# One residual block of four conditional layers on one core: the third matrix's pieces loaded ahead of the ring's blocks, table stores spread over two units, the last sum of U2 D3 moved, and the first couple's plain product cut into parts of 136 and 256 columns

## The reference

```
x = x + x W0^T + 2 * sum over the top 2 of 8 experts of gate_e * (x A_e^T) B_e^T
x = x + (per sequence of 64 tokens: C^T x, C a 64x64 matrix chosen by an id)
x = x + (x B2[id]^T) A2[id]^T            (rank 16, one of 64 adapters)
x = x + x W3^T + b + 2 * (x A3[id]) B3[id]   (rank 16, one of 32 adapters)
```

## Time and profile before

| | |
|---|---|
| median of three runs | 892.26 us |
| profiled execution | 890.0 us, its span 888.2 us |
| VectorE, ScalarE, GpSimd busy | 693.1, 379.6, 243.6 us |
| mean granted TensorE clock | 0.989 of full |
| HBM traffic | 193 GB/s over the span |

### The profile page before, as it was taken

How to read it: one execution, slowest core, us unless ns; L and a number is a source line. 1 busy time by engine, 2 the same in 40 slices (tenths; PEclk the granted TensorE clock), 3 DMA queues, 4 the chain that set the end, 5 groups by cost and what they waited for, 6 DMA issues and landing times.

```text
span 888.2 us, 15396 instructions
## 1 busy us (share of the span) xinstructions
PE 865.9 (97%) x4572; PEld 798.4 (90%) x4572; DVE 693.1 (78%) x1900; ACT 379.6 (43%) x859; POOL 243.6 (27%) x343
## 2 busy tenths in 40 slices
PE   8989999999999998899999999999999999999997
PEld 7868788888888887799999999999999999999997
DVE  5894444665565724799999999999999999999996
ACT  5562333344445732434434434434434345345343
POOL 1410100000001114415415415425325325335230
PEclk9989999999999998999999999999999999999999
DMA  7718666669687765546666655666566566566564
GB/s 260 262 61 187 173 184 167 192 187 304 226 277 241 175 166 113 155 149 185 192 181 182 196 180 183 182 185 189 173 174 194 173 188 193 174 185 186 180 189 144
DMA packets 120969, 166.24 MB, mean 187 GB/s; under 512 B 33718, under 2 KB 80566, under 8 KB 120886
## 3 DMA queue, kind: packets, MB, share of 16 engines
q1 hardware_dynamic: 120886, 165.26, 62.9%
HBM read 128.78 MB, written 42.73 MB: 193 GB/s over the span
## 4 chain that ended last, share of the span: by engine, by line
PE 72%; DVE 17%; issue 4%; DMA 3%; ACT 2%; SPq 2%; POOL 1%; DVEq 0%; POOLq 0%
PE ps_w L2125 12%; PE ps_d L2046 10%; PE ps_d L2125 10%; PE ps_o L2024 9%; PE ps_d L2117 8%; PE ps_o L2046 8%; PE ps_o L2138 4%; DVE stat_lo L1482 4%; PE ps_d L2132 3%; PE ps_s L2024 2%; PE ps_o L2162 2%; DVE CT_raw L1497 1%; PE ps_w L2132 1%; DVE rows_lo L1482 1%; DVE spare_f L1794 1%
## 5 line engine op out<-in xcount | busy, mean ns | idle before, releaser
L1482 DVE TENSOR_TENSOR stat_lo<-stat_raw,stat_hi 128x512 fp32r<-128x512 f32 (+1 forms) x150 | 148.9, 1008 | 56.2 <-ACT stat_hi L1026 46.3
L1026 ACT ACTIVATE stat_hi<-stat_raw 128x512 fp32r<-128x512 f32 (+1 forms) x150 | 115.5, 789 | 73.6 <-DVE stat_raw L1500 41.2
L875 POOL TENSOR_TENSOR stat_raw<-stat_raw,ident 128x128 f32<-128x128 f32 x36 | 25.0, 697 | 266.5 <-DMA stat_raw<-stat 266.5
L2117 PE MATMUL ps_d<-w_hi,stat_hi 128*128 128x392 f32 x256 | 87.2, 341 | 0.8 <-DVE y_lo L1482 0.8
L2117 PE MATMUL ps_d<-w_hi,stat_lo 128*128 128x392 f32 x256 | 87.0, 340 | 0.0
L2117 PE MATMUL ps_d<-w_lo,stat_hi 128*128 128x392 f32 x256 | 86.9, 340 | 0.0
L918 POOL TENSOR_TENSOR w_lo<-mdraw,w_hi 128x512 fp32r<-128x512 f32 x32 | 41.7, 1304 | 160.7 <-ACT w_hi L1026 160.7
L2024 PE MATMUL ps_o<-chunk_hi,stat_hi 128*128 128x512 f32 x168 | 65.7, 391 | 1.0 <-DVE stat_lo L1482 0.5
L2024 PE MATMUL ps_o<-chunk_hi,stat_lo 128*128 128x512 f32 x168 | 65.4, 389 | 0.0
L2024 PE MATMUL ps_o<-chunk_lo,stat_hi 128*128 128x512 f32 x168 | 65.4, 389 | 0.0
L1026 ACT ACTIVATE rows_hi<-rows_raw 128x512 fp32r<-128x512 f32 x52 | 32.6, 627 | 59.0 <-DMA rows_raw<-u 28.6
(11 more groups left out here) (284 smaller groups left out, 2520.8 us busy)
## 6 DMA issues: line engine op xcount, KB each, us to landing
up<-tu SPq DMA_DIRECT2D x124, 256.0 KB, 4.3
stat_raw<-x SPq DMA_DIRECT2D x33, 512.0 KB, 3.2
mdraw<-t SPq DMA_DIRECT2D x120, 136.0 KB, 2.4
out<-outb SPq DMA_DIRECT2D x30, 512.0 KB, 4.3
stat_raw<-stat SPq DMA_DIRECT2D x52, 256.0 KB, 3.2
stat_raw<-stat SPq DMA_DIRECT2D x26, 512.0 KB, 5.0
rows_raw<-x SPq DMA_DIRECT2D x30, 256.0 KB, 3.2
chunk_raw<-mov SPq DMA_DIRECT2D x24, 256.0 KB, 6.0
```

Of the source, the lines that this page charges most:

```text
L875: return nc.gpsimd.tensor_tensor(out=own, in0=own, in1=ident[:, :], op=ALU.add)
L1026: return nc.scalar.activation(dst, src, ACT.Copy)
L1482: return nc.vector.tensor_tensor(out=dst, in0=src, in1=rounded.bitcast(F32), op=ALU.subtract)
L2117: last = nc.tensor.matmul(plain_bank(t)[:, 0:WCOLS], rows[a][:, k, :], w[c][:, k, :], start=k == 0 and m == 0, stop=k == KB - 1 and m == l ...
```

## The change

M3's pieces are issued at the groups 0, 1 and 2: eight, four and four, each time behind the ring's block. Its steps are spread from group 0 on: ten of the twelve over the groups 0 to 6, and in group 0 and 1 the ring's blocks are split two at once; from group 2 on the block of two groups later is split, on VectorE and ScalarE, ahead of the group's steps. The language bias (`languages`) goes from before the groups to after unit 1. The stores of the D3 table are issued two before and two after the loads of A12 and A22, at unit 0 and again at unit 1; `store_mb(2)` goes to unit 1; the twelve `store_own` go to units 2 and 3, three before and three after. The last sum of U2 D3 is a function of its own, `hidden_total`, called a few instructions later.

In the first couple the plain product of each tile is made as `heads` (136 columns) and `others` (256 columns), each of 24 matmuls, so that heads need nothing from the tables. Two of the sums S of the first couple are kept in rooms of their own, and no longer wait for the table's stores (`st_md[1]`). The order on all engines is new:

```diff
-    M3_EACH = 3
+    M3_LOADED = [8, 12, 16]
-    M3_AT_GROUP = {2: M3_STEPS[0:1], 3: M3_STEPS[1:3], 4: M3_STEPS[3:5], 5: M3_STEPS[5:6], 6: M3_STEPS[6:8], 7: M3_STEPS[8:10]}
-    M3_IDENTITIES = {1: 0, 3: 1, 4: 2, 5: 3}
+    M3_AT_GROUP = {0: M3_STEPS[0:2], 1: M3_STEPS[2:3], 2: M3_STEPS[3:4], 3: M3_STEPS[4:6], 4: M3_STEPS[6:7], 5: M3_STEPS[7:9],
+                   6: M3_STEPS[9:10]}
+    M3_IDENTITIES = {0: 0, 1: 1, 2: 2, 3: 3}
...
-                for n in range(g * M3_EACH, min((g + 1) * M3_EACH, len(M3_PIECES))):
-                    load_m3(n)
+                if g < len(M3_LOADED):
+                    for n in range(M3_LOADED[g - 1] if g > 0 else 0, M3_LOADED[g]):
+                        load_m3(n)
...
-                if u == 0:
-                    for n in range(STORES):
-                        store_md(2, n)
-                    store_mb(2)
+                if u < 2:
+                    store_md(2, 4 * u)
+                    store_md(2, 4 * u + 1)
...
             def first():
+                x1_lo(0)
+                gate(0)
                 s_lo(0, 0)
+                s_lo(0, 2)
+                hgT_lo(0)
+                gate(1)
+                b03_lo()
                 s_lo(0, 1)
-                x1_lo(0)
                 s_lo(0, 3)
-                s_lo(0, 2)
-                b03_lo()
-                gate(0)
                 hidden_sum(0)
+                hidden_total(0)
...
+            def heads(t):
+                rows = x0 if t % 2 == 0 else x1
+                for k in range(KB):
+                    for m, (a, c) in enumerate(PASSES):
+                        last = nc.tensor.matmul(plain_bank(t)[:, 0:HL], rows[a][:, k, :], w[c][:, k, 0:HL],
+                                                start=k == 0 and m == 0, stop=k == KB - 1 and m == len(PASSES) - 1,
+                                                skip_group_check=True)
+                return last
...
             def first():
                 a, b = 0, 1
+                heads(a).then_inc(pe_hl, 1)
                 winograd(ps_w, A11, B11, True).then_inc(pe_p[0], 1)
                 winograd(ps_x, A12, B21, True).then_inc(pe_p[1], 1)
+                heads(b).then_inc(pe_hl, 1)
+                gated_rows(a)
                 winograd(right_bank(0), S_first[0], T1, True).then_inc(pe_p[4], 1)
                 winograd(ps_w, S_first[1], T2, False).then_inc(pe_p[5], 1)
+                others(a).then_inc(pe_rest, 1)
+                hidden_product(a)
                 experts(a, plain_bank(a)[:, HL:WCOLS], YP).then_inc(pe_xp, 1)
                 experts(a, ps_x[:, 0:SH], YL).then_inc(pe_La, 1)
                 winograd(ps_w, S_first[2], T3, False).then_inc(pe_p[6], 1)
                 gated_rows(b)
+                others(b).then_inc(pe_rest, 1)
                 experts(b, plain_bank(b)[:, HL:WCOLS], YP).then_inc(pe_xp, 1)
                 experts(b, ps_x[:, 0:SH], YR, True).then_inc(pe_Rb, 1)
                 hidden_product(b)
                 winograd(ps_w, A22, T4, False).then_inc(pe_p[3], 1)
                 experts(b, ps_w[:, 0:SH], YL).then_inc(pe_Lb, 1)
                 winograd(right_bank(0), S_first[3], B22, False).then_inc(pe_p[2], 1)
                 experts(a, right_bank(0)[:, 0:SH], YR).then_inc(pe_Ra, 1)
```

More of the change, by code:

```diff
@@ L737, in _ @@
                     load_stat(B0_NUMBER + 2)
+                if u < 2:
+                    store_md(2, 4 * u + 2)
+                    store_md(2, 4 * u + 3)
+                elif not u2:
+                    for n in range((u - 2) * OWN_EACH + OWN_EACH // 2, (u - 1) * OWN_EACH):
+                        store_own(n)
+                if u == 1:
+                    store_mb(2)
                 if u2:
@@ L1631, in _, with languages @@
                 first_lo(k)
[L1633 to L1640, removed]
[L1641 to L1644 removed]
+            def languages():
+                dve.wait_ge(ld_ids, 16 * 4)
+                dve.wait_ge(pool_const, CONSTS)
+                lang_at = lang_sb[:, :].rearrange("p (t b) -> p b t", b=BT)
+                for b in range(BT):
+                    rows = slice(b * TB, (b + 1) * TB)
+                    nc.vector.tensor_copy(lang_f[rows, :], lang_at[rows, b, :]).then_inc(dve_set, 1)
+                dve.wait_ge(dve_set, BT)
+                nc.vector.tensor_tensor(out=rbias[:, :, :], in0=lang_f[:, :, None].to_broadcast([P, TILES, EXPERTS]),
+                                        in1=iota_e[:, None, :].to_broadcast([P, TILES, EXPERTS]), op=ALU.is_equal).then_inc(dve_set, 1)
+                dve.wait_ge(dve_set, BT + 1)
+                nc.vector.tensor_scalar(rbias[:, :, :], rbias[:, :, :], LANG_BIAS, None, ALU.mult).then_inc(dve_set, 1)
+                dve.wait_ge(dve_set, SETS)
             def x0_lo(j):
@@ L1693, in _ @@
                 unit(u)
+                if u == 1:
+                    languages()
             for k in range(HALF_KB):
@@ L1888, in Rb_part @@
                     dve.wait_ge(pe_mix, 2 * j)
-                part = part3[:, 0:SH] if at(j, 0) else part1[:, :]
-                nc.vector.tensor_tensor(out=yraw[1][:, YR], in0=right_bank(j)[:, 0:SH], in1=part,
+                nc.vector.tensor_tensor(out=yraw[1][:, YR], in0=right_bank(j)[:, 0:SH], in1=part1[:, :],
                                         op=ALU.add).then_inc(dve_Rb_raw, 1)
@@ L1953, in fore @@
                 hgT_lo(a)
+                hidden_total(a)
                 hidden_rows(b1)
@@ L1970, in step @@
                 Rb_raw(j)
+                hidden_total(b)
                 hidden_rows(a)
@@ L2205, in ranks3, with others @@
                     ranks(h3T, up3, t, n).then_inc(pe_out[n], 1)
+            def heads(t):
[6 more added lines that the diff above has]
+                return last
+            def others(t):
+                rows = x0 if t % 2 == 0 else x1
+                for k in range(KB):
+                    for m, (a, c) in enumerate(PASSES):
+                        last = nc.tensor.matmul(plain_bank(t)[:, HL:WCOLS], rows[a][:, k, :], w[c][:, k, HL:WCOLS],
+                                                start=k == 0 and m == 0, stop=k == KB - 1 and m == len(PASSES) - 1,
+                                                skip_group_check=True)
+                return last
             def first():
```

166 lines of the change are left out of this document (85 added, 81 removed).

## The result

The kernel after takes 875.53 us (median of 4 runs, 875.24 to 876.11), the kernel before, in 4 runs beside them, 891.58 (890.34 to 892.68). The ratio is 0.9821, 95% interval 0.9804 to 0.9838: 16.05 us less. The forecast was 12.4 less, 879.9. The profiled execution after took 875.24 us, its span is 873.5: in the profiles the difference is 14.74 us. The other 1.3 us are scatter: before's profiled execution lies 1.6 us under its median, after's 0.3.

What follows compares the result with a forecast made beforehand. TensorE's matmuls bound the kernel, so only its waits and half-clock stretches can be won: 8.5 (units 0 and 1) + 3.9 (first couple) = 12.4 us off 892.26, giving 879.9 us, range 875.5 to 884.5.

Steps and rivals of the forecast that it cites:

- Term 1: Units 0 and 1: waits of 4.00 and 1.74 us and 2.78 of half clock go; 8.5 less, bounds 4.5 and 8.5.
- rival D: Groups: blocks 4 to 8 each come some 2 us late, clock halves after each; slower, 900; chance 0.05.
- Rival A: Groups: M3's pieces land as late as before, ring blocks stand behind unrun steps; about 7 off, 885; chance 0.1.
- the later stores cannot do worse per load than before: Units 2 and 3: three copies ahead of a load instead of four, so nothing is lost there.
- Term 2: First couple: new matmul order gains 4.8 us, less clock and mix costs; 3.9 us less, bounds 2 to 6.
- the chain that the forecast named: First couple's end: SyncE's id reads, 2.4 us each, delay tile 2's w load; couple 1 starts at 363.0.
- Rival C: First couple: SyncE's reads overlap or are quick, 9 us gained, 17 off in all, 875; chance 0.1.
- a half chance: Couple 1: the clock falls at the last wait, costing up to 1.7 us; priced at 0.5.
- Rival B: First couple gives nothing: new waits and three clock falls cost what the old ones did; 883.7; chance 0.1.
- 0.2 us on VectorE, off the path: Moved last sum of U2 D3, `hidden_total`: only 0.2 us of VectorE work, nothing gained.

Runs made afterwards that it cites:

- run 7: Kernel after with M3's pieces again issued three per group, steps as early as after: 885.26 us, 9.7 more than after.
- run 2: Kernel before with only the spread of the table stores: 891.5 us, ratio 0.9996 to the kernel before.
- run 10: Kernel after with the table stores put back where they were before the change: 874.83 us, ratio 0.9824 to the kernel before.
- run 6: Kernel after with the second half of each unit's stores and copies issued behind the load of A11: 874.04 us, 1.5 under after.
- run 1: Kernel before with only the M3 part (pieces ahead, steps spread from group 0, languages moved): 883.33 us, 8.2 less.
- run 9: Kernel after with late second-half stores, SyncE's first couple reordered, x0 loaded behind the small rows, tile 2's table load ahead of tile 3's ids: 870.57 us.
- run 4: Kernel before with only the last sum of U2 D3 moved out of hidden_sum to behind hgT: 887.55 us, 4.0 less.
- run 5: Kernel after with the last sum of U2 D3 put back into hidden_sum: 881.57 us, 6.0 more than after.
- run 8: Kernel after with SyncE's first couple reordered: tile 2's ids read during small-row stores, tile 1's small rows loaded ahead of mix and bias: 874.35 us.
- run 3: Kernel before with only the new first couple, last sum still in hidden_sum: 886.72 us, 4.8 less.

## Why the prediction was right, and where it was short

**Term 1, start: right in its mechanism, 0.6 us less.** GpSimd stood for the first four pieces until 18.41 (the forecast had the fourth in at about 17), and VectorE's first sum stands at 19.70 (18.6 forecast, 25.74 in the earlier trace rows). Only one block of the ring cost TensorE more than before, 0.26 us at 41.47, and the sums of unit 0 stand at 53.93 (forecast 51.9, before 57.62). Timeline of VectorE after; the steps of the earlier trace rows begin 6.0 us earlier and end 3.7 us earlier. Before, they had four blocks of the ring among them, now five, at 1.2 to 1.5 us each; the forecast's own list has the fifth, but the argument against rival D (31.9 us of work in 33.3) counts four, so the 1.4 us of room that it saw weren't there:

```profile
19.70 0.69 DVE L1517 TENSOR_TENSOR CT_raw<-CT_raw,C_raw 128x512 f32<-128x512 f32 x1 [1.05 <-POOL CT_raw L909]
...
40.19 1.23 DVE L1502 TENSOR_TENSOR stat_lo<-stat_raw,stat_hi 128x1024 fp32r<-128x1024 f32 x1 [0.20 <-ACT stat_hi L1042]
...
53.93 0.68 DVE L1517 TENSOR_TENSOR stat_raw<-stat_raw 128x512 f32<-128x512 f32 x1
```

The sums' 2.0 us of lateness used up the 1.7 us of slack that the forecast saw before unit 0, whose own start was 0.6 late, and no wait came. So the cover is thin: in the seven profiles with this order of the groups, unit 0 starts anywhere from 57.35 to 58.61 us. Run 7 is the counter-proof: without the early loads the same step order costs 9.7 us. Rival A had priced that at 5.4 (7 instead of 12.4 off), with 4.9 us of waits where 7.6 came; that run 7's time is nevertheless A's 885 is luck, since it has the gain of the last sum too, which A knew as little as the forecast did.

**Term 1, unit 1: right, and worth nothing.** The 1.74 us came to the hundredth, yet "the later stores cannot do worse per load than before" is the step that failed. The sentence counted the copies ahead of one pair of loads, A12 and A22. The load behind these, A11 of the unit after next, now has six copies a unit ahead of it where it had four, three of them directly. Timelines of ScalarE and TensorE after, in the units 3 and 4: the half block of the next unit comes so late that the copy which frees TensorE's bank is late too, the picture of the earlier trace rows in other units:

```profile
122.26 0.63 ACT L1042 ACTIVATE stat_hi<-stat_raw 128x512 fp32r<-128x512 f32 x1 [3.55 <-DMA stat_raw<-stat]
122.79 0.58 ACT L1042 ACTIVATE wpart<-ps_o 128x512 f32<-128x512 f32 x1
...
142.29 0.63 ACT L1042 ACTIVATE stat_hi<-stat_raw 128x512 fp32r<-128x512 f32 x1 [4.29 <-DMA stat_raw<-stat]
142.83 1.07 ACT L1042 ACTIVATE wpart<-ps_d 128x512 f32<-128x512 f32 x2
```

```profile
123.52 0.47 PE L2078 MATMUL ps_o<-CB_hi,stat_hi 128*128 128x512 f32 x1
```

Of the 1.39 us lost, 0.74 is the wait in unit 4. The other 0.65 is counted as busy, and nearly all of it lies at the same place: the matmul behind this copy and the next one start 0.99 us late together in unit 4 (the 0.74 included), 0.26 in unit 3 (0.40 and 0.31 us from start to start instead of 0.227, at 123.52) and about 0.1 in unit 2. So the late half block, and not a general slowing of the matmuls, is what the units 3 and 4 lose by. Spreading alone nets nothing (runs 2 and 10), and the units are all whole once the second half stands behind the load (run 6). The copies aren't the only thing that makes the half block late: run 1 has none of them moved and loses 0.59 us in unit 3.

**Term 2, the first couple: right.** All times from the start of heads(0), the forecast's from its own clock less 326.95:

| | forecast | after |
|---|---|---|
| 24 heads | 2.7 | 2.64 |
| experts(0), wait | 18.85, 1.2 | 18.75, 0.86 |
| w of tile 1, wait | 0.5 | 0.35 |
| experts(1), wait | 27.45, 2.0 | 27.64, 1.89 |
| load of tile 2's rows issued | 29.85 | 30.03 |
| couple 1, wait | 36.05, 1.6 | 36.39, 1.43 |

Timeline of TensorE after, the first and last of the heads and the four waits. From the first of 24 to the row behind the last of them: (323.09 - 320.45)/24 = 0.110 us.

```profile
320.45 0.22 PE L2243 MATMUL ps_d<-w_hi,stat_hi 128*128 128x136 f32 x1
...
323.09 0.40 PE L2157 MATMUL ps_w<-B_hi,stat_hi 128*128 128x416 f32 x1
...
339.20 0.39 PE L2164 MATMUL ps_d<-b_hi,hgTa_hi 128*128 128x256 f32 x1 [0.86 <-POOL b_lo L948]
...
343.12 0.38 PE L2252 MATMUL ps_d<-w_hi,stat_hi 128*128 128x256 f32 x1 [0.35 <-POOL w_lo L935]
...
348.09 0.36 PE L2164 MATMUL ps_d<-b_hi,hgTb_hi 128*128 128x256 f32 x1 [1.89 <-POOL b_lo L948]
...
356.84 0.42 PE L2149 MATMUL ps_d<-w_hi,stat_hi 128*128 128x392 f32 x1 [1.43 <-issue]
```

The value chosen for 136 columns, 0.112, was near the upper end, and 0.110 came. That the weight load is what stays fits this, but no run changes the load itself. Of the two sections that the forecast quoted from the Trainium skill, "TensorE: Matmul & The Clock Gate", this row agrees with "LDWEIGHTS (loading the stationary operand)" (columns/1.2, an estimate of 107 ns for 128 columns), not with "Back-to-back issue gap" (81 ns per pair).

The end of the couple is the chain that the forecast named. Timeline of SyncE's issues, and of ScalarE and GpSimd: two reads of ids, 2.8 and 3.2 us from issue to issue, then the load, and its data 4.2 us later. The profile puts TensorE's wait down to "issue" and not to `w_lo`, the forecast's releaser; but GpSimd's `w_lo` ends at 356.74, 0.1 us before TensorE starts:

```profile
344.53 0.37 SPq L675 DMA_DIRECT2D stat_raw<-x  x1
347.33 0.34 SPq L687 DMA_DIRECT2D stat_raw<-x  x1
350.48 0.87 SPq L630 DMA_DIRECT2D mdraw<-t  x2
```

```profile
354.70 0.63 ACT L1042 ACTIVATE w_hi<-mdraw 128x512 fp32r<-128x512 f32 x1 [2.53 <-DMA mdraw<-t]
355.48 1.26 POOL L935 TENSOR_TENSOR w_lo<-mdraw,w_hi 128x512 fp32r<-128x512 f32 x1 [7.53 <-ACT w_hi L1042]
```

Rival C (the couple below 34 us because SyncE is quick) needed the reads taken out of this chain. Run 9 does that, and the couple takes 32.63.

**Term 2, the clock: a half chance that fell the other way.** 0.5 us was taken for a fall behind the last wait and 0.5 for couple 1's mix. After, the clock never fell while TensorE had work, though it waited 1.89 and 1.43 us; couple 1 became 0.62 shorter. Nothing in the rows told the two cases apart, so that it fell this way is luck. Rival B fell with it. (4.8 less these 1.0 is 3.8, not the forecast's 3.9.)

**"0.2 us on VectorE, off the path": the largest miss.** The step that failed put the moved addition at 0.2 us and off the path; both are wrong. Moved from `hidden_sum` to behind `hgT_lo` (in a couple's second tile to behind `Rb_raw`), it is worth 2.9 us in the profile's couples 2 to 14, 4.0 alone (run 4), 6.0 when put back (run 5, by medians; 4.1 by profiles). It is one addition a tile, and by itself it takes 0.17 us. But in its old place, in the first tile of a couple, it took 1.03 us: it starts 0.3 us behind the start of GpSimd's `w_lo` and ends with it. GpSimd and VectorE before:

```profile
410.57 1.30 POOL L918 TENSOR_TENSOR w_lo<-mdraw,w_hi 128x512 fp32r<-128x512 f32 x1 [1.33 <-ACT w_hi L1026]
410.88 1.03 DVE L1818 TENSOR_TENSOR spare_f<-spare_f 32x32 f32<-32x32 f32 x1
...
420.69 0.29 DVE L1482 TENSOR_TENSOR hgTa_lo<-ps_s,hgTa_hi 128x128 fp32r<-128x128 f32 x1
```

VectorE after, in the same tile:

```profile
408.77 0.29 DVE L1502 TENSOR_TENSOR hgTa_lo<-ps_s,hgTa_hi 128x128 fp32r<-128x128 f32 x1 [0.53 <-ACT hgTa_hi L1042]
408.98 0.17 DVE L1846 TENSOR_TENSOR spare_f<-spare_f 32x32 f32<-32x32 f32 x1
```

This holds for every one of the 32 additions in each trace. Before, 15 start while `w_lo` runs; all of them end within 0.05 us of its end (14 take 1.02 to 1.03 us, one that starts later 0.63), and the other 17 take 0.18. After, the first tiles' take 0.17 or 0.18, and now 14 of the second tiles start beside `w_lo` and take 1.11, where TensorE does not wait behind them. That the one operation holds up the other is read from these times; no run moves `w_lo` alone.

So 0.86 us left VectorE's list ahead of hgT's split, and they are found again in these rows: VectorE has 0.53 us of idle in front of `hgTa_lo` where it had none, and `hgTa_lo` starts 0.31 us behind ScalarE's `hgTa_hi` instead of 0.64. Behind the split stands the gate of the couple's second tile; its `gexp` on ScalarE comes just in front of the copy of P6 (`part`), which P7 waits for. ScalarE and TensorE before:

```profile
420.05 0.28 ACT L1026 ACTIVATE hgTa_hi<-ps_s 128x128 fp32r<-128x128 f32 x1 [1.18 <-PE ps_s L2174]
...
422.98 0.20 ACT L1274 ACTIVATE gexp<-gdiff 128x1 f32<-128x1 f32 x1 [2.65 <-DVE gdiff L1725]
423.09 0.50 ACT L1026 ACTIVATE part<-ps_w 128x416 f32<-128x416 f32 x1
```

```profile
422.10 0.28 PE L2132 MATMUL ps_d<-b_hi,hgTa_hi 128*128 128x256 f32 x1
...
423.01 0.60 PE L2168 MATMUL ps_s<-u2s,d3m 128*64 128x64 f32 x8
423.64 0.46 PE L2125 MATMUL ps_w<-T_hi,rows_hi 128*128 128x416 f32 x1
```

After, in the same place:

```profile
408.46 0.28 ACT L1042 ACTIVATE hgTa_hi<-ps_s 128x128 fp32r<-128x128 f32 x1 [2.00 <-PE ps_s L2206]
...
411.11 0.20 ACT L1295 ACTIVATE gexp<-gdiff 128x1 f32<-128x1 f32 x1 [2.37 <-DVE gdiff L1751]
411.22 0.50 ACT L1042 ACTIVATE part<-ps_w 128x416 f32<-128x416 f32 x1
```

```profile
410.53 0.28 PE L2164 MATMUL ps_d<-b_hi,hgTa_hi 128*128 128x256 f32 x1
...
411.45 0.60 PE L2200 MATMUL ps_s<-u2s,d3m 128*64 128x64 f32 x8
411.89 0.43 PE L2157 MATMUL ps_w<-T_hi,rows_hi 128*128 128x416 f32 x1
```

P6 ends where the experts' first matmul starts. From there to the copy: 0.99 us before, 0.69 after. From the hidden product to P7: 0.63 before, 0.44 after. The forecast does not name this wait. The view of waits has only 0.8 us of it, in four places: a pause of 0.2 us between pipelined matmuls is mostly counted as a longer start, not as a wait. The windows show it: of the 2.91 us, 0.96 were idle time and 1.95 counted as busy. What should have been looked at is the distance between the starts of couples, which varied by 0.4 us, and how long the addition took in the place that it was moved from.

**The sum.** 8.5 + 3.9 = 12.4 became 6.5 + 5.1 + 3.1 = 14.7 in the profiles. Errors of -2.0, +1.2 and +3.1 us add up to the 2.3 that the profiles differ from the forecast by. So the time is inside the range for a partly wrong reason, and only just: 875.53 is at its lower end, 875.5. It is rival C's time, 875, but not C's mechanism, since the couple took 36.39 us and not under 34. Without the term that was taken for nothing the kernel takes 881.57 (run 5), 1.7 over the forecast.

## What to carry to other kernels

Price an edit on an engine that isn't the bound by what the instruction takes in its place and by whether the engine has idle time just there, not by its usual length and the engine's share over the span: an addition of 0.17 us took 1.03 beside another engine's work, on a list without a gap, and moving it was worth 0.22 us a couple on average (2.91/13). When traffic is moved away from one late load, follow it to the load that it now stands before, since a spread that nets nothing looks like a success in the unit where it starts. And where a serial engine's own reads (ids into registers) end a chain, doing them while it waits anyway is worth pricing: together with the earlier loads of x0 and of the small rows it took the couple from 36.39 to 32.63 us (run 9), where the reordering of the matmuls had taken it from 40.88 to 36.39.

## What the runs showed of the hardware that was not expected

- A matmul of 136 columns starts every 0.110 us, one of 256 every 0.117: between these two widths nearly nothing is saved.
- An addition of 32x32 on VectorE took 0.17 or 0.18 us, but 1.02 to 1.12 when it started 0.2 to 0.3 us behind the start of GpSimd's 1.3 us `w_lo`: it ended with it, in all 28 such cases of the traces before and after.
- The granted clock fell to half level in or behind single waits of 1.37 us (run 8), 1.94 (run 6), 2.18 (run 3), 2.29 (run 10), 2.85 and 5.09 (run 7), but not behind 1.89 and 1.43 in the kernel after, nor behind 2.50 before experts(1) in run 6. No length of wait divides the two.
- A fall inside the first couple cost little: in run 10 it lasts 6.83 us, and the first two couples take 71.24 us together against 71.17 after. The waits of 1.43 us ahead of couple 1 and of 0.79 in it, which the kernel after has, don't occur there: part of what the clock cost would have been waited anyway.
- The runs of the kernel before scatter over 888 to 894 us, those of the kernel after and of run 6 within 1 us. In run 7, which has long waits in the groups, they scatter over 9.
